# State-space stage: the skip term enters the bank by transposes, and GpSimd applies the skip weights

## The reference

```python
def step(state, inp):
    dA_t, dt_t, B_t, C_t, x_t = inp
    dBx = jnp.einsum('bh,bn,bhp->bhpn', dt_t, B_t, x_t)
    state = state * dA_t[:, :, None, None] + dBx
    return (state, jnp.einsum('bhpn,bn->bhp', state, C_t))
...
y = jnp.moveaxis(y, 0, 1) + Dskip[None, None, :, None] * xs
y = y.reshape(Bb, Ll, D_INNER)
y = _rmsnorm(y * jax.nn.silu(z), norm_w)
return y @ W_out.T
```

## Time and profile before

| | us |
|---|---|
| three runs | 4015.73, 4015.79, 4019.7 |
| their median | 4015.79 |
| the profiled execution | 4015.51 |
| its span in the profile | 4013.8 |
| its mean granted TensorE clock | 0.985 |

### The profile page before, as it was taken

The page is one execution under the profiler, slowest core; times in us unless marked ns, Lnnn a source line. Parts: engine busy times, 40 slices in busy tenths (PEclk is TensorE's granted clock), DMA queues, the critical chain, the costliest instruction groups (busy, mean ns, idle before and its releaser), DMA issues. The chain is left out here.

```text
span 4013.8 us, 109330 instructions
## 1 busy us (share of the span) xinstructions
PE 3818.1 (95%) x35786; PEld 3005.5 (75%) x35786; DVE 2927.0 (73%) x7397; ACT 2792.8 (70%) x6292; POOL 1900.5 (47%) x1728
## 2 busy tenths in 40 slices
PE   8999899999979999897999989999999989998999
PEld 6777788888746666685666668888888877776777
DVE  7888655555479999657999965767676768886665
ACT  5555455555579999756999975777777768884333
POOL 5555322222268888536777763333333331112444
PEclk9999899999989999999999999999999989999999
DMA  1000100000100000100000011000000000000000
GB/s 30 19 20 20 52 7 6 6 7 6 42 9 8 8 8 8 26 20 10 8 8 8 8 29 35 1 0 0 0 0 0 0 2 4 4 4 6 12 12 13
DMA packets 118477, 46.71 MB, mean 12 GB/s; under 512 B 92256, under 2 KB 117088, under 8 KB 117728
## 3 DMA queue, kind: packets, MB, share of 16 engines
q1 hardware_dynamic: 118368, 45.30, 4.3%
HBM read 24.36 MB, written 4.19 MB: 7 GB/s over the span
## 5 line engine op out<-in xcount | busy, mean ns | idle before, releaser
L1102 POOL TENSOR_TENSOR l_rc<-l_rc,l_rs 128x1024 f32<-128x1024 f32 x128 | 303.6, 2372 | 201.4 <-DVE l_rs L1294 201.4
L1169 ACT ACTIVATE l_prob<-l_prob,l_mx 128x128 f32<-128x128 f32 x1024 | 312.0, 389 | 0.0
L670 POOL TENSOR_TENSOR ca_prob<-ca_prob,ca_sm 128x1232 f32<-128x1232 f32 x64 | 143.9, 2248 | 299.5 <-DVE ca_sm L836 299.5
L1780 POOL TENSOR_TENSOR mb_steps<-w_upto,mb_dta 128x1024 f32<-128x1024 f32 x64 | 121.4, 1897 | 345.9 <-DVE mb_dta L2048 345.9
L1194 PE MATMUL l_qk_ps<-w_local,l_hT 128*128 128x512 f32 x512 | 248.5, 609 | 13.3 <-DVE l_rs L1294 11.2
L1096 POOL TENSOR_TENSOR l_prob<-l_prob,l_sm 128x1024 f32<-128x1024 f32 x128 | 242.8, 1897 | 16.9 <-DVE l_sm L1280 16.9
L1079 POOL TENSOR_TENSOR l_rc<-l_rc,l_ss 128x1024 f32<-128x1024 f32 x128 | 243.4, 1902 | 12.5 <-POOL l_rc L1102 4.5
L1939 PE MATMUL mb_x_ps<-w_wx,mb_xT 128*128 128x256 f32 x1024 | 236.8, 384 | 0.0
L382 ACT ACTIVATE la_ef<-la_feat,la_fbias 128x1024 f32<-128x1024 f32 x128 | 135.8, 1112 | 120.2 <-PE la_feat L441 120.2
L2515 POOL TENSOR_TENSOR mo_hid<-mo_hid,mo_gate 128x1024 f32<-128x1024 f32 x64 | 121.7, 1902 | 199.9 <-DVE mo_hid L2661 199.9
L346 POOL TENSOR_SCALAR la_ef<-la_ef,la_high,la_low 128x1024 f32<-128x1024 f32 x128 | 151.0, 1190 | 133.0 <-ACT la_ef L382 133.0
(11 more groups left out here) (350 smaller groups left out, 11849.9 us busy)
## 6 DMA issues: line engine op xcount, KB each, us to landing
la_xin<-in_x SPq DMA_DIRECT2D x64, 64.0 KB
la_xT<-in_x_T SPq DMA_DIRECT2D x64, 64.0 KB, 1.8
l_h<-lt_y SPq DMA_DIRECT2D x128, 32.0 KB
lt_quad<-lt_y SPq DMA_DIRECT2D x32, 128.0 KB
out_x<-k_x SPq DMA_DIRECT2D x64, 64.0 KB, 1.5
l_h<-lt_y SPq DMA_DIRECT2D x128, 31.8 KB
lt_quad<-lt_y SPq DMA_DIRECT2D x32, 127.0 KB
ca_ctxT<-in_ctx_T SPq DMA_DIRECT2D x128, 19.2 KB
```

The costliest lines, as they stand in the source:

```text
L1102: gp.tensor_tensor(wide(rc[l][:]), wide(rc[l][:]), wide(rs[l][:]), ALU.add).then_inc(*pool_sum.did("rot"))
L1169: ex = sc.activation(p[:, a, j], p[:, a, j], ACT.Exp, bias=mx[l][:, a, j:j + 1])
```

## The change

The eight skip products with `ddiag` are gone, and so is `ddiag` itself, with the GpSimd instruction in `prepare` that made it. In its place GpSimd multiplies the activated values by the skip weights (`dcol`, one per head) to a new buffer `skip` (128 x 512, twice), as the last thing in its step, for the batch that is at `PROJ`. TensorE turns `skip` into the bank `y_ps` with four transposes of 128 x 128 (one for each pair of heads), the first of which starts the bank; then the eight products of `xdt` with `decay` are added. TensorE has one more wait ahead of y, for `skip`. The two buffers `skip` take as much room as `ddiag` did.

```diff
--- before.py
+++ after.py
@@ -1570,7 +1570,7 @@
     nw, ow = state["nw"], state["ow"].rearrange("p (k a) -> p k a", k=DIRS)
     xrow = state["xrow"].rearrange("p (k j e) -> p k j e", k=DIRS, j=TAPS)
     crow = state["crow"].rearrange("p (j e) -> p j e", j=TAPS)
-    nega, dcol = steps["nega"], steps["dcol"]
+    nega = steps["nega"]
     NFETCH = 4 * 16
     with ExitStack() as stack:
         m = Memory(nc, stack, "cw")
@@ -1588,9 +1588,6 @@
                                      pattern=[[-sign, T]], channel_multiplier=sign).then_inc(masks, 1)
                     gp.affine_select(out=g.upto[:, k], in_=g.upto[:, k], compare_op=ALU.is_ge, fill=0.0, base=0,
                                      pattern=[[sign, T]], channel_multiplier=-sign).then_inc(masks, 1)
-                gp.wait_ge(g.fetched, NFETCH)
-                gp.tensor_tensor(g.ddiag[:], g.ident[:].unsqueeze(1).to_broadcast([T, HEADS, T]),
-                                 dcol.unsqueeze(2).to_broadcast([T, HEADS, T]), ALU.mult).then_inc(masks, 1)
 
             @block.scalar
             def _(sc):
@@ -1680,12 +1677,12 @@
     with ExitStack() as stack:
         m = Memory(nc, stack, "mb")
         wx, wbc, wz, wdt, wout = g.wx, g.wbc, g.wz, g.wdt, g.wout
-        ddiag, upto, beyond = g.ddiag, g.upto, g.beyond
+        upto, beyond = g.upto, g.beyond
         steps_in = g.steps_part
         cw = steps_in["cw"].rearrange("p (k a j) -> p k a j", k=DIRS, a=4)
         cbx = steps_in["cbx"].rearrange("p (k e) -> p k e", k=DIRS)
         cbbc = steps_in["cbbc"].rearrange("p (k a) -> p k a", k=DIRS)
-        dtb, nega, projb = steps_in["dtb"], steps_in["nega"], steps_in["projb"]
+        dtb, nega, projb, dcol = (steps_in[n] for n in ("dtb", "nega", "projb", "dcol"))
         eps = m.sb("eps", [128, 1])
         r, xn = both(m, "r", [T, C]), both(m, "xn", [T, C])
         stats, mv, rstd = both(m, "stats", [T, 6]), both(m, "mv", [T, 2]), both(m, "rstd", [T, 3])
@@ -1698,7 +1695,7 @@
         pre = both(m, "pre", [DS, NSH, T])
         zs = both(m, "zs", [128, DIRS * PAIRS, T])
         steps = both(m, "steps", [T, HEADS, T])
-        gm, xdt = both(m, "gm", [T, DIRS, T]), both(m, "xdt", [T, DIRS, DI])
+        gm, xdt, skip = both(m, "gm", [T, DIRS, T]), both(m, "xdt", [T, DIRS, DI]), both(m, "skip", [T, DIRS, DI])
         decay = both(m, "decay", [T, HEADS, T])
         u, usq = both(m, "u", [128, DIRS * PAIRS, T]), both(m, "usq", [128, DIRS * PAIRS, T])
         uq = both(m, "uq", [128, DIRS, T])
@@ -1732,6 +1729,7 @@
         pool_norm = Stage(m.sem("pool_norm"), "xp xr")
         pool_dt = Stage(m.sem("pool_dt"), "steps")
         pool_seg = Stage(m.sem("pool_seg"), "xdt")
+        pool_skip = Stage(m.sem("pool_skip"), "xd")
         pool_out = Stage(m.sem("pool_out"), "uq")
         NORM, TURN, PROJ, SEG, OUT = range(5)
         ORDER = [*SHIFTED, *[c for c in ((0, 0), (0, 1), (1, 0), (1, 1)) if c not in SHIFTED]]
@@ -1740,6 +1738,7 @@
         two = lambda ap: ap.rearrange("p a c -> p (a c)")
         by_dir = lambda ap: ap.rearrange("p (k h) t -> p k h t", k=DIRS)
         per_step = lambda ap: ap.rearrange("p (k h) -> p k h", k=DIRS).unsqueeze(3).to_broadcast([T, DIRS, NH, T])
+        heads = lambda ap: ap.rearrange("p k (h e) -> p (k h) e", e=HD)
         per_head = lambda ap: ap.unsqueeze(2).to_broadcast([T, DIRS, NH, T])
 
         with nc.Block() as block:
@@ -1753,7 +1752,7 @@
                 gp.memset(eps[:], LN_EPS).then_inc(zeroed, 1)
                 for l in (0, 1):
                     gp.memset(xT[l][:], 0.0).then_inc(zeroed, 1)
-                for stage in (pool_norm, pool_dt, pool_seg, pool_out):
+                for stage in (pool_norm, pool_dt, pool_seg, pool_skip, pool_out):
                     stage.start(gp)
 
                 def step(at):
@@ -1766,7 +1765,6 @@
                                          ).then_inc(*pool_out.did("uq"))
                     b = at(SEG)
                     if b:
-                        heads = lambda ap: ap.rearrange("p k (h e) -> p (k h) e", e=HD)
                         gp.wait_ge(*act_proj.at("sx", b))
                         gp.wait_ge(*vec_dt.at("dt", b))
                         gp.wait_ge(*pe_seg.at("y", b, ago=2))
@@ -1785,6 +1783,13 @@
                         gp.tensor_tensor(r[b.lane][:], r[b.lane][:], projb, ALU.add).then_inc(*pool_norm.did("xp"))
                         gp.wait_ge(*pool_norm.at("xp", b))
                         gp.tensor_tensor(one(b), one(b), r[b.lane][:], ALU.add).then_inc(*pool_norm.did("xr"))
+                    b = at(PROJ)
+                    if b:
+                        gp.wait_ge(*act_proj.at("sx", b))
+                        gp.wait_ge(*pe_seg.at("y", b, ago=2))
+                        gp.tensor_tensor(heads(skip[b.lane][:]), heads(xs[b.lane][:]),
+                                         dcol.unsqueeze(2).to_broadcast([T, HEADS, HD]), ALU.mult
+                                         ).then_inc(*pool_skip.did("xd"))
 
                 pipeline(gp, g.NB, OUT + 2, step)
 
@@ -1950,14 +1955,16 @@
                         te.wait_ge(*act_proj.at("sx", b))
                         te.wait_ge(*vec_seg.at("m", b))
                         te.wait_ge(*vec_out.at("u", b, ago=1))
+                        te.wait_ge(*pool_skip.at("xd", b))
                         te.wait_ge(*pool_seg.at("xdt", b))
                         place = lambda h: y_ps[64 * (h % 2):64 * (h % 2) + 64, T * (h // 2):T * (h // 2) + T]
                         cols = lambda h: slice(HD * (h % NH), HD * (h % NH) + HD)
                         for pair in range(HEADS // 2):
-                            for h in (2 * pair, 2 * pair + 1):
-                                te.matmul(place(h), xdt[l][:, h // NH, cols(h)], decay[l][:, h], start=True, stop=False)
-                            for h in (2 * pair, 2 * pair + 1):
-                                mm = te.matmul(place(h), xs[l][:, h // NH, cols(h)], ddiag[:, h], start=False, stop=True)
+                            k, first = pair // PAIRS, 128 * (pair % PAIRS)
+                            te.matmul(y_ps[:, T * pair:T * pair + T], skip[l][:, k, first:first + 128], g.ident[:],
+                                      start=(pair == 0), stop=False, is_transpose=True)
+                        for h in range(HEADS):
+                            mm = te.matmul(place(h), xdt[l][:, h // NH, cols(h)], decay[l][:, h], start=False, stop=(h >= HEADS - 2))
                         mm.then_inc(*pe_seg.did("y"))
                     b = at(TURN)
                     if b:
@@ -2683,7 +2690,6 @@
         g.steps_w, g.steps_part = kept.weights("steps", "steps")
         g.wx, g.wbc = kept.sb("wx", [C, 2, 4, 256]), kept.sb("wbc", [C, 2, 4, 2, 128])
         g.wz, g.wdt, g.wout = kept.sb("wz", [C, 2, 2, 128]), kept.sb("wdt", [C, 8]), kept.sb("wout", [128, 2, 2, C])
-        g.ddiag = kept.sb("ddiag", [T, 8, T])
         g.beyond, g.upto = kept.sb("beyond", [T, 2, T]), kept.sb("upto", [T, 2, T])
         with ExitStack() as early:
             cross = Memory(nc, early, "wc", "right")
```

## The result

The changed kernel takes 3993.3 us, the median of 4 runs (3992.33 to 3993.97), beside 4015.8 (4015.01 to 4019.7) for the kernel before on the same chip: a ratio of 0.9942 with a 95% interval of 0.993 to 0.9954, or 22.5 us less. The forecast was 3988.0 in a range of 3981 to 3998. The direction and the range held, and 4.9 us of the 27.4 worked out did not come.

What follows compares the result with a forecast made beforehand. TensorE's own list of passes was taken to bound the state-space stage. Removing 0.873 and adding 0.44 us saves 0.43 a batch, 27.4 us over 63 batches: 4015.8 to 3988 us, range 3981 to 3998.

Steps and rivals of the forecast that it cites:

- (a): TensorE's y step: removing the eight skip products, four groups of 0.218 us, saves 0.873 us a batch.
- (b): TensorE ahead of y: four added 128x128 transposes at 0.11 us each cost 0.44 us a batch.
- (c): TensorE's seams: transposes to y replaces z to y, 0.20 us either way, so 0 net.
- (d): Bounds on one transpose adding into y's bank: 0.110 us from below, 0.33 from above if nothing overlapped; 0.11 taken.
- rivals 2, 3 and 4: 2: adding transposes don't overlap, 4044 us, 3%; 3: cost like products, 4016 us, 2%; 4: cost a quarter, 3975 us, 2%.
- (e): GpSimd's added skip multiply takes 1.04 us a batch, fits the gap before uq, and costs nothing.
- (h): VectorE beside GpSimd's new pass: contention taken as 0, upper bound 0.21 us a batch on the way to dta.
- (f): Loops through other engines: steps-to-seg slack falls from 1.07 to 0.64 us, xT-to-bc to some 0.8; neither becomes the bound.
- prediction's own signs of being wrong: Transposes over 0.15 us apart, seg or xT product starting right at its releaser, or the mask multiply growing.
- Rival 5: A loop through steps or xT, or alternating buffers, keeps 0.1 to 0.3 us a batch: 3994 to 4007 us, 6%.
- Rival 1: GpSimd's new pass holds up VectorE's mask multiply by 1.04 us, making steps late: 4014 us, no change, 3%.
- (g): Setup: dropping the diagonal matrix removes one GpSimd pass of 2.06 us, hidden behind ScalarE, so 0.

Runs made afterwards that it cites:

- Experiment 1: The changed kernel with GpSimd's xdt multiply moved to the end of the step, behind the skip pass, so both multiplies precede uq; 3988.3 us.
- Experiment 8: The changed kernel with both GpSimd multiplies ahead of uq, and the four transposes made twice, eight in a row; 4017.5 us.
- experiments 4 and 5: 4: the changed kernel without GpSimd's skip pass, TensorE turning xs itself, 3994.7 us; 5: the kernel before with that pass added, output unused, 4016.3 us.
- experiment 3: The changed kernel with the small softplus operation reading one input from PSUM, its minimum re-formed with an add, GpSimd's order kept; 3989.2 us.
- experiment 9: The changed kernel with TensorE's loop running four batches to a trip instead of two, the other engines keeping two; 3992.8 us.
- experiment 6: The kernel before with an unused half-width GpSimd multiply between uq and xdt, so that xdt runs later; 4017.9 us.

## Why the prediction was right, point by point

The direction, the range and the main mechanism, a TensorE list shorter by 0.43 us a batch, held. That the loss stayed at 5 us was not foreseen: the hold that caused it was in no term.

- **(a), (b), (c), TensorE's list: right.** 0.11 us a transpose, 0.20 for the seam, 1.67 from z to the turn. Experiment 1 shows the sum itself, 26.6 us over 63 batches (743.9 - 717.3) and 27.8 against the kernel before of its call, where 27.4 was worked out. Experiment 8 settles (d): the bound of 0.33 and rivals 2, 3 and 4 are out.
- **(e), the GpSimd pass is free: right** (experiments 4 and 5), and it lay in the gap that was named. What (e) passed over is in its last sentences: of a later `uq` and `xdt` it asked only who *reads* them. Nobody does, early; but someone runs beside `xdt`. Before, `xdt` ended at 2908.30 + 1.04 = 2909.34, 0.09 after the operation of line 2079 began:

```profile
2909.25 0.17 DVE L2079 SCALAR_TENSOR_TENSOR mb_dts<-mb_dts 128x8 f32<-128x8 f32 x1
```

The softplus hangs on TensorE's dt product; `xdt` hangs on `uq`, and so on ScalarE, which didn't become faster. With TensorE's list shorter the two slid together: 0.71 us of `xdt` are left in the changed kernel when that operation starts (2910.32 - 2909.61), and 0.38 in the same place where nothing is held (experiment 3, 2918.05 - 2917.67). So part of the hold is its own doing.

- **(h), a term that was mis-sized.** (h) had at most 0.21 of contention a batch, on the mask multiply. The mask multiply is untouched, 1.23 us as before. The contention came on an operation of 128x8 that the argument didn't list, and it was 0.55 us, 2.6 times the bound: a held operation doesn't slow by a share, it waits for the rest of the other one. The earlier trace rows shows that already: the multiply that starts at 3263.49 met only the last 3263.85 - 3263.49 = 0.36 us of `xdt`, and it took 0.21 longer, the rest less 0.15. In the changed kernel the rest is 0.71 and the operation 0.57 longer, the rest less 0.14. So 0.21 was the price of one short overlap and no upper bound.
- **(f), the other one.** (f) had 0.64 us of slack left after the change. It took the 1.11 us from `steps` to the seg product, less 0.04. But the weight load waits for `steps` too, and it starts with the turn, 0.16 ahead of the product:

```profile
2905.69 0.33 PE L1967 MATMUL mb_out_ps<-k_ident,mb_xn 128*128 128x128 f32 x1
2905.69 0.79 PEld L1886 LDWEIGHTS mb_seg_ps<-mb_steps,w_beyond 128*128 128x128 f32 x4
```

That is 2905.69 - 2904.74 = 0.95 us after `steps`. In experiment 9 weights 0.11 behind the turn already cost 0.05 us. By the weights some 0.5 us was left (0.51 in experiment 1), an estimate from these rows, and the hold of 0.55 uses that up. Behind it stands a feedback, read from the waits and not tested by itself: a held softplus makes VectorE's convolution taps late, ScalarE waits for them (1.92 us in the changed kernel, 1.45 before), VectorE waits for `zs` in turn, and with ScalarE `uq` and the next `xdt` come later. What is left unpaid is 722.3 - 717.3 = 5.0 us over 63 batches, 0.08 a batch. Experiments 1 and 3 each take the hold away in a different way, and both bring it back (3988.3 and 3989.2).

- One of the prediction's own signs of being wrong did come: the seg weights start right at their releaser, 0.05 us after `steps`. The time stayed in the range even so.
- **Rival 5 came true in kind, below its size**: the loop through `steps` kept 0.08 us a batch, not 0.1 to 0.3. Rival 1 was the right mechanism with the wrong pair: `xdt` in place of the new pass, the softplus in place of the mask multiply.
- The Trainium skill ("SBUF — State Buffer", Who interferes with whom) says that a VectorE instruction with two SBUF inputs contends with a GpSimd instruction that reads SBUF, and that one with at most one SBUF input doesn't, unless it runs in a two-port mode, which `tensor_scalar` can enter. The traces agree with the first half and with the exemption: 1.04 us for a 0.17 us operation in experiment 6, 0.16 in experiment 3. The exemption has its limit in this case as well: line 2092 in experiment 6, a `tensor_scalar` with one SBUF tensor, takes 1.12 us beside `xdt` and 0.35 without. Which mode it ran in, no run here shows. The prediction cited the rule for two inputs and applied it only to `u` and to the mask multiply.
- **(g)** No run removes `ddiag` alone; in experiment 1 the whole came out as worked out without it (27.8 against 27.4). GpSimd's +67 us came as +62, 2.06 of the difference being `ddiag` itself.

Left open: whether the loop that holds the changed kernel at 11.465 goes round through TensorE at every batch, or whether the circle of VectorE, ScalarE, `uq` and `xdt` has that period by itself. No run separates these. The best version is experiment 1; 3988.3 is 5.0 us below the changed kernel, and the ranges touch at one run.

## What to carry to other kernels

When the bounding engine gets shorter, every pair of engines slides against each other. List which GpSimd passes come beside which VectorE operations with two SBUF inputs, the tiny ones too, and beside a `tensor_scalar` from SBUF to SBUF (line 2092 in experiment 6). Price an overlap at the rest of the GpSimd pass, not at a share of it. Such a hold is free while slack lies behind it (experiment 6), so compare it with the slack that the change leaves, and put GpSimd's long passes where VectorE waits anyway; it can be an edit of queue order alone (experiment 1).

Pay attention to the distance from a releaser to its weight load, not to the table of waits. In the changed kernel the seg weights start 0.05 or 0.17 us after `steps`, batch by batch, where it was 0.95, and the table names that wait only twice in the stage. Count slack from that load, not from the product behind it.

## What the runs showed of the hardware that was not expected

- An operation of 128x8 elements with two SBUF inputs takes as long as what is left of the GpSimd multiply beside it: 0.17 us alone, 0.74 and up to 1.07 beside it. In the changed kernel it ends 0.01 to 0.04 us after that multiply in every batch in which they meet.
- With one input in PSUM (and an add for the minimum) it runs at 0.16 us inside the GpSimd multiply.
- A `tensor_scalar` of 128x128 that reads one tensor from SBUF is held too: 0.35 us alone, up to 1.14 beside the multiply (experiment 6).
- Float32 transposes that don't start a bank's sum did not add to what earlier transposes had put there, while products issued after them add (experiment 8, by its output). It wasn't tried further.
- The number of batches in a trip of the loop moves single batches by 0.1 us and the mean by nothing (722.3 us for 63 batches either way).
